# Second attention's way in: a projection in two parts, shared out over DVE, ACT and POOL

## The reference

```python
qkv = jnp.einsum('bsd,df->bsf', x, Wqkv) + bqkv          # 256 + 64 + 64 columns
q = qkv[..., :256].reshape(b, s, 32, 8)
k = qkv[..., 256:320].reshape(b, s, 8, 8)                # repeated 4 times
v = qkv[..., 320:].reshape(b, s, 8, 8)                   # repeated 4 times
attn = softmax(einsum('bqhd,bkhd->bhqk', q, k) / sqrt(8))
out = einsum('bhqk,bkhd->bqhd', attn, v).reshape(b, s, 256) @ Wo + bo
```

## Time and profile before

| | us |
|---|---|
| median of 3 runs (lowest, highest) | 669.72 (668.78, 669.96) |
| the profiled execution | 669.68 |
| its span, first to last instruction | 667.8 |
| TensorE, DVE, ACT, POOL busy | 617.4, 404.4, 325.1, 213.2 |
| mean granted TensorE clock | 0.986 of 2.4 GHz |
| maxima of the scores on DVE, L1744, 256 | 157.6 |
| exps on ACT, L1505, 256 | 138.0 |

### The profile page before, as it was taken

One profiled execution on the slowest core, in us unless ns is written; L12 is line 12 of the kernel. 1 busy time (PEld: TensorE's weight loads), 2 busy tenths in 40 slices (PEclk: granted clock), 3 DMA queues, 4 the chain that ended last, 5 costly groups with the idle time before them and its releaser, 6 DMA issues.

```text
span 667.8 us, 11795 instructions
## 1 busy us (share of the span) xinstructions
PE 617.4 (92%) x4298; PEld 408.0 (61%) x4298; DVE 404.4 (61%) x929; ACT 325.1 (49%) x645; POOL 213.2 (32%) x312
## 2 busy tenths in 40 slices
PE   3999999999999988799978999999999999989990
PEld 2887887887888785366665544444444445546660
DVE  4526705632760587533366999989998954743336
ACT  4523423433332224133215589898988875523322
POOL 5870561282073154513333031201010100331331
PEclk9999999999999999899989999999999999999996
DMA  6000200300199992222379994000000000031213
GB/s 220 33 1 33 96 1 20 107 1 1 38 283 299 78 314 77 78 58 81 105 237 346 303 180 3 1 1 2 2 1 2 1 2 1 9 104 55 81 56 126
DMA packets 69000, 57.40 MB, mean 86 GB/s; under 512 B 21520, under 2 KB 64400, under 8 KB 68944
## 3 DMA queue, kind: packets, MB, share of 16 engines
q1 hardware_dynamic: 66736, 50.60, 31.2%
q0 software_dynamic: 2208, 6.05, 2.5%
HBM read 30.78 MB, written 25.85 MB: 85 GB/s over the span
## 4 chain that ended last, share of the span: by engine, by line
PE 73%; DVE 16%; DMA 3%; ACT 3%; issue 2%; POOL 1%; SPq 1%; ACTq 0%; POOLq 0%; DVEq 0%
PE psum L303 9%; PE psum L305 8%; PE psum L304 8%; PE psum L1289 8%; PE psum L1634 8%; DVE mx L1744 7%; PE psum L1606 5%; PE psum L1318 5%; PE psum L1594 5%; PE psum L1619 3%; PE psum L1213 2%; DVE stat L666 2%; PE psum L1564 2%; PE psum L1282 2%; PE psum L1199 1%
## 5 line engine op out<-in xcount | busy, mean ns | idle before, releaser
L1744 DVE TENSOR_REDUCE mx<-psum 128x1 f32<-128x512 f32 x256 | 157.6, 681 | 17.6 <-PE psum L1606 17.5
L1505 ACT ACTIVATE pr<-psum 128x512 f32<-128x512 f32 x256 | 138.0, 598 | 27.9 <-PE psum L1619 26.1
L1634 PE MATMUL psum<-pr,vals 128*32 128x256 f32 x1024 | 77.6, 389 | 0.0
L1619 PE MATMUL psum<-qT,kT 32*128 32x512 f32 x256 | 76.6, 494 | 0.7 <-ACT pr L1505 0.7
L1606 PE MATMUL psum<-kT,qT 32*128 32x512 f32 x256 | 67.7, 488 | 1.7 <-ACT qT L1472 0.7
L1289 PE MATMUL psum<-w_gu,xgT 128*128 x120 | 56.4, 592 | 0.0
L624 POOL DMA_INDIRECT routed_y<-yr,xg x30 | 28.7, 958 | 86.1 <-DVE yr L876 85.5
L1606 PEld LDWEIGHTS psum<-kT,qT 32*128 32x128 f32 x256 | 26.3, 181 | 43.9 <-issue 21.4
L1546 POOL CAST mp<-mx 128x16 bf16<-128x16 f32 x16 | 3.1, 196 | 150.5 <-DVE mx L1744 150.5
L867 DVE SCALAR_TENSOR_TENSOR h<-psum,xg,sg 128x256 f32<-128x256 f32 x30 | 14.5, 484 | 49.8 <-ACT sg L1046 49.8
L1046 ACT ACTIVATE sg<-psum,xg 128x256 f32<-128x256 f32 x30 | 14.2, 474 | 60.4 <-PE psum L1289 60.4
(11 more groups left out here) (214 smaller groups left out, 1406.6 us busy)
## 6 DMA issues: line engine op xcount, KB each, us to landing
sorted_x<-zeros SPq DMA_DIRECT2D x2, 9088.0 KB, 39.2
w_gu<-in_L_ffn_gate_w SPq DMA_DIRECT2D x16, 256.0 KB, 6.2
w_gu<-in_L_ffn_up_w SPq DMA_DIRECT2D x16, 256.0 KB, 6.3
w_d<-in_L_ffn_down_w SPq DMA_DIRECT2D x16, 256.0 KB, 6.6
xg<-sorted_x SPq DMA_DIRECT2D x30, 129.0 KB, 2.2
wk_f<-in_L_attn_Wk SPq DMA_DIRECT2D x4, 512.0 KB, 5.2
wq_f<-in_L_attn_Wq SPq DMA_DIRECT2D x4, 512.0 KB, 6.0
wv_f<-in_L_attn_Wv SPq DMA_DIRECT2D x4, 512.0 KB, 3.7
```

The costliest lines, as they stand in the source:

```text
L1505: nc.scalar.activation(pr[d % 3][:, j], s2_bank(d, j), ACT.Exp, scale=SCALE).then_inc(exp_ready, 1)
L1619: mm(s2_bank(d, j), kT[n // GH][rows, kc * P:(kc + 1) * P], qT2[n % 2][rows, :], start=True, stop=True).then_inc(s2_made, 1)
L1634: last = mm(ps[AV_BANK][j * VW:(j + 1) * VW, cols], vals[:, n // NKV * TB + kc, n % NKV // GH * GH + j, :], pr[d % 3][:, j, cols], start=( ...
L1744: v.tensor_reduce(mx[n % 2][:, t, j:j + 1], s1_bank(c, j), AX.X, ALU.max, negate=True).then_inc(max_read, 1)
```

## The change

The projection of the first sequence's four tiles is split. project_first makes 128 columns: the keys (64) and the first eight heads' queries (64). DVE takes these with the bias (take_first), ACT makes their high parts, and DVE both low parts (first_low), the last two between the statistics of x; stats_x(1) moves behind the takes. project_rest makes the other 192 query columns and the 64 value columns, for tile 0 after the turn of q1, for tiles 1 to 3 in steps 0 to 2, in place of keep-warm matmuls. ACT copies them without the bias (take_rest); POOL adds the bias, makes high and low parts, and adds the values' bias as it copies them. In steps 3 to 6 ACT in place of DVE takes the second sequence's tiles (take), again without the bias, which POOL adds. complete(1) is split in three, in steps 3, 4 and 5. The second half's turned x goes through banks 6 and 7 in place of 4 and 6, and the turn in step 2 waits for its copies. Ahead of it all 25 keep-warm units become 18, a wait and 8. qkv and wqkv get 512 columns per tile, so that one access pattern reaches both parts of the first 128 columns; stack_hi and stack_lo get a range of heads.

```diff
+HALF = NQ * HD
+FH = 2 * GH
+FQ = FH * HD
...
-        TURN_X = ((4, 5, 6, 7), (0, 1, 0, 1), (0, 1, 4, 6), (0, 1, 0, 1))
+        TURN_X = ((4, 5, 6, 7), (0, 1, 0, 1), (0, 1, 6, 7), (0, 1, 0, 1))
...
                     else:
                         mark(ins)
-            def stats_x(half):
+            def stats_x(half, between=None):
                 for i in range(TB):
                     dve.wait_ge(dve_chain, sums_from[half] + i + 1)
                     tile_stats(x, half * TB + i)
+                    if between:
+                        between(i)
                 close_stats(0, half)
...
-            close_x(1, 1)
-            l1_y = dve_l1(dve, link, mark, settle, y_tiles, close_stats, sum_x)
+            sum_x(1, 1)
+            l1_y = dve_l1(dve, link, mark, settle, y_tiles, close_stats, sum_x, stats_x)
             stats_x(0)
             for t in range(TB, NT):
...
-            def complete(p):
-                for t in range(NT):
+            def complete(p, tiles=range(NT)):
...
             pe.wait_ge(y_ready, NT + 1)
-            keep_warm(25, 2)
+            keep_warm(18, 2)
+            pe.wait_ge(rstd_ready[1], 5)
+            keep_warm(8, 2)
             pe.wait_ge(var_ready[0], 10)
             keep_warm(5, 2)
...
+        REST_BANK = (3, 4, 3, 4)
...
+        def first_of(ap):
+            return ap.rearrange("p (a n) -> p a n", a=2)[:, :, 0:FQ]
...
-            def hi_parts(b, t):
-                act.wait_ge(qkv_ready, b * TB + t + 1)
-                stack_hi(nc.scalar, b, t, "k").then_inc(k_hi_made[b], 1)
-                stack_hi(nc.scalar, b, t, "q").then_inc(q_hi_made[b], 1)
+            def first_hi(t):
+                act.wait_ge(first_ready, t + 1)
+                stack_hi(nc.scalar, 0, t, "k").then_inc(k_hi_made[0], 1)
+                stack_hi(nc.scalar, 0, t, "q", (0, FH)).then_inc(q_hi_made[0], 1)
+            def take_rest(t):
+                act.wait_ge(rest_made, t + 1)
+                nc.scalar.activation(qkv[:, t, FQ:HALF], ps[REST_BANK[t]][:, 0:HALF - FQ], ACT.Copy)
+                nc.scalar.activation(qkv[:, t, KEND:QKV], ps[REST_BANK[t]][:, HALF - FQ:HALF], ACT.Copy).then_inc(qkv_ready, 1)
+            def take(t):
+                act.wait_ge(qkv_made, t + 1)
+                nc.scalar.activation(qkv[:, t, 0:QKV], ps[QKV_BANK[t]][:, 0:QKV], ACT.Copy).then_inc(qkv_ready, 1)
             act.wait_ge(l1_consts, L1_CONSTS)
             for t in range(TB):
-                hi_parts(0, t)
+                first_hi(t)
             for what in FIRST:
                 copy_turn(what)
+            take_rest(0)
             normalise(2, 1)
+            take_rest(1)
             for c in range(END):
                 d = c - LAG
+                if c == 1:
+                    take_rest(2)
                 if c == 2:
                     turn_copy(2, 2)
                     turn_copy(2, 3)
-                    complete(1)
+                if c == QKV_AT:
+                    take_rest(3)
+                if QKV_AT <= c < min(QKV_AT + TB, LAG):
+                    take(TB + c - QKV_AT)
+                    if c + 1 < QKV_AT + TB:
+                        complete(1, range(NT)[(c - QKV_AT) * NT // 3:(c + 1 - QKV_AT) * NT // 3])
                 n = (c - 12) // TB if c % TB == 0 and c >= 12 else -1
                 if 0 <= n < NG:
                     act.wait_ge(av_done, (n + 1) * TB)
...
                     if 0 <= d < STEPS:
                         act.wait_ge(s2_made, s2_no(d, j) + 1)
                         nc.scalar.activation(pr[d % 3][:, j], s2_bank(d, j), ACT.Exp, scale=SCALE).then_inc(exp_ready, 1)
+                if LAG <= c < QKV_AT + TB:
+                    take(TB + c - QKV_AT)
...
+            def add_bias(t, cols):
+                g.tensor_tensor(qkv[:, t, cols], qkv[:, t, cols], bqkv[:, cols], ALU.add).then_inc(biased, 1)
             for t in range(TB):
-                pool.wait_ge(q_hi_made[0], t + 1)
-                stack_lo(g, 0, t, "q").then_inc(q_stacked[0], 1)
+                pool.wait_ge(qkv_ready, t + 1)
+                add_bias(t, slice(FQ, HALF))
+                pool.wait_ge(biased, t + 1)
+                stack_hi(g, 0, t, "q", (FH, NQ)).then_inc(rest_hi, 1)
+                pool.wait_ge(rest_hi, t + 1)
+                stack_lo(g, 0, t, "q", (FH, NQ)).then_inc(q_stacked[0], 1)
             def values(b):
                 tiles = slice(b * TB, (b + 1) * TB)
-                g.tensor_copy(vals[:, tiles, :, 0:HD],
-                              qkv[:, tiles, KEND:QKV].rearrange("p t (g d) -> p t g d", d=HD)).then_inc(vals_ready, 1)
+                g.tensor_tensor(vals[:, tiles, :, 0:HD], qkv[:, tiles, KEND:QKV].rearrange("p t (g d) -> p t g d", d=HD),
+                                bqkv[:, KEND:QKV].rearrange("p (g d) -> p g d", d=HD).unsqueeze(1).to_broadcast([P, TB, NKV, HD]),
+                                ALU.add).then_inc(vals_ready, 1)
             values(0)
             def second_batch(t):
                 pool.wait_ge(qkv_ready, TB + t + 1)
+                add_bias(TB + t, slice(0, KEND))
+                pool.wait_ge(biased, TB + t + 1)
...
+            def columns(o, t, cols):
+                for c in range(KC):
+                    last = mm(o, xT[:, c, t * P:(t + 1) * P], cols(wqkv[:, c]), start=(c == 0), stop=(c == KC - 1))
+                return last
+            def project_first(t):
+                pe.wait_ge(xT_ready, 4 * 2 + t // 2 + 1)
+                columns(ps[QKV_BANK[t]][:, 0:2 * FQ], t,
+                        first_of).then_inc(qkv_made, 1)
+            def project_rest(t):
+                if t >= 2:
+                    pe.wait_ge(qkv_ready, t - 1)
+                columns(ps[REST_BANK[t]][:, 0:HALF - FQ], t, lambda w: w[:, FQ:HALF])
+                columns(ps[REST_BANK[t]][:, HALF - FQ:HALF], t, lambda w: w[:, KEND:QKV]).then_inc(rest_made, 1)
             def project_qkv(t):
                 pe.wait_ge(xT_ready, 4 * 2 + t // 2 + 1)
-                if t >= TB:
-                    pe.wait_ge(qkv_ready, t if t == NT - 1 else TB)
-                for c in range(KC):
-                    last = mm(ps[QKV_BANK[t]][:, 0:QKV], xT[:, c, t * P:(t + 1) * P], wqkv[:, c],
-                              start=(c == 0), stop=(c == KC - 1))
-                last.then_inc(qkv_made, 1)
+                pe.wait_ge(qkv_ready, t if t == NT - 1 else TB)
+                columns(ps[QKV_BANK[t]][:, 0:QKV], t, lambda w: w[:, 0:QKV]).then_inc(qkv_made, 1)
             def turn(what):
                 n = TURNS.index(what)
...
                     wait_bank(pe, what)
                 elif n >= 2:
                     wait_read(pe, TURNS[n - 1])
+                    pe.wait_ge(xT_ready, 4 * 2 + 4)
                 else:
-                    pe.wait_ge(qkv_ready, TB)
+                    pe.wait_ge(first_stacked, TB)
                 into = ps[bank_no(what)]
                 kind, i = what
                 b, u = divmod(i, 2 if kind == "k" else NKV)
...
                 elif kind == "k":
                     pe.wait_ge(k_stacked[b], TB)
                 else:
-                    pe.wait_ge(q_stacked[b], TB)
+                    if i * GH < FH:
+                        pe.wait_ge(first_stacked, TB)
+                    else:
+                        pe.wait_ge(q_stacked[b], TB)
                     if kind == "q2":
                         pe.wait_ge(max_ready, i + 1)
                 for t in range(TB):
...
             turn_x(2, range(2))
             for t in range(TB):
-                project_qkv(t)
-            pe.wait_ge(qkv_ready, TB)
-            keep_warm(3, 3)
+                project_first(t)
+            keep_warm(4, 3)
             turn(FIRST[0])
-            keep_warm(4, 3)
+            keep_warm(2, 3)
             turn(FIRST[1])
+            project_rest(0)
             for c in range(END):
                 d = c - LAG
                 if c == 2:
                     turn_x(2, range(2, 4))
                 if c < STEPS:
                     scores1(c, 0)
-                if c < QKV_AT:
-                    keep_warm(2, 3)
+                if c < 2:
+                    project_rest(c + 1)
                 if 0 <= d < STEPS:
                     scores2(d, 0)
                 if 0 <= d - 2 < STEPS and (d - 2) % TB:
...
                         if what[1] == NG - 1:
                             keep_warm(2, SPARE)
                         turn(what)
-                if c < QKV_AT:
-                    keep_warm(2, 3)
+                if c < 2:
+                    keep_warm(2, AV_BANK)
+                if c == 2:
+                    project_rest(3)
                 if 0 <= d < STEPS:
...
-            def take(t):
+            def take_first(t):
                 dve.wait_ge(qkv_made, t + 1)
-                v.tensor_tensor(qkv[:, t, :], ps[QKV_BANK[t]][:, 0:QKV], bqkv[:], ALU.add).then_inc(qkv_ready, 1)
-            def key_lo(t):
```

(45 more changed lines are left out.)

3 lines of the change are left out of this document (1 added, 2 removed).

## The result

| | before | changed |
|---|---|---|
| median of 20 runs each (lowest, highest), us | 674.02 (668.78, 677.6) | 676.41 (673.13, 680.23) |
| ratio, 95% interval | | 1.0057 (1.0038, 1.0075) |
| the profiled execution, us | 669.68 | 676.85 |
| its span, us | 667.8 | 675.1 |
| its mean granted clock | 0.986 | 0.970 |

The ratio is the one on record; the medians differ by 2.4 us and the means by 3.1 ± 1.3 us. Of all runs told of here one, the slowest of e3, lay over 1.5% above the fastest of its kernel, and is left out of e3's ratio and means.

A forecast was written before the change was run, and what follows sets the result against it. The stretch from the way in to the first loop steps was taken as serial, TensorE carrying 73% of the span. A 2.5 us lead, all but 0.1 lost to q2's late copy, gave 669.68 - 0.1, set at 669.5; range 668.3 to 671.1.

The forecast's parts named there:

- The base: Whole kernel: profiled execution 669.68 us and median 669.72 before the change, both given the same forecast, 669.5.
- The way in: First projections to first scores: smaller pieces bring first scores to 359.35 against 362.19, a lead of 2.85 us.
- rival 3: DVE's low parts at the way in cost 0.35 each, first_stacked at 358.5, total 671.0 us; chance 0.05.
- Steps 0 to 2: Loop start: steps 0 and 1 take 2.27 us each, with project_rest 1.0 and warmers 0.43; step 2 ends at 367.6.
- The stall on the copy: Step 5: ACT copies q2 only after take(6) and three tiles of x; scores2(0, 0) at 377.85, TensorE idle about 2 us.
- the lead: Time gained: 2.85 us at first scores, 2.5 at the end of project_qkv(6), 0.1 left at scores2(0, 0).
- What follows "is as before": After scores2(0, 0): exps, project_qkv(7) and maxima at the same distances as before, first weigh at 385.2.
- the gap on the way in: TensorE idle 1.6 us from 355.4, after four warmers and before turn k; full clock expected to hold.
- Rival 2: Clock falls after the 1.6 us idle at 355.4, losing 1.9 us in steps 0 and 1: 671.4 us; chance 0.09.
- two counter-examples: Against the clock falling: stretches busy 1.14 and 0.44 of 2.00 us, read as 1.56 idle, kept the full clock.
- DVE relieved of the takes: Steps 3 to 6: DVE loses four takes of 0.55 us; the time saved is idle, about 2 us before its 27th maximum.
- Rival 1: Step 5: q2's copy does not come behind project_qkv(6), so the 2.5 us lead is kept: 667.2 us; chance 0.08.

The follow-up runs named there:

- e3: Kernel before, with ACT in step 5 waiting for tile 6's projection and completing four tiles of x before copying q2: ratio 1.0084, mean +4.6 ± 1.7 us.
- e1: Changed kernel, but in step 5 ACT copies q2 before taking tile 6 and completing x: ratio 1.0011 to the kernel before.
- e2: Changed kernel with nine keep-warm units filling TensorE's idle time just ahead of scores2(0, 0): ratio 1.0015 to the kernel before, mean +1.6 ± 0.9 us.
- e5: e4 with DVE again taking the second sequence's tiles with the bias, POOL adding none to them: ratio 0.9986 to the kernel before.
- e4: e1 with x completed in steps 3 and 4, four tiles each: ratio 0.9981 to the kernel before, first weigh at 33.90 against 34.98 in e1.
- e6: e4 with weights ordered queries, values, keys, so a tile's rest is one block of 256 columns: ratio 0.9978 to the kernel before.

## Why the prediction was wrong, point by point

- **The base: the larger part of the miss.** The forecast was 669.5, the measured median 676.41, 6.9 us more. 4.3 of them are the kernel before itself, whose median went from 669.72 in three runs to 674.02 in twenty; I had taken three runs within 0.2% as its spread, and it spreads over 1.4%, by the clock. The other 2.6 are the change's: forecast 0.2 below the base's median, it came 2.4 above, and that by itself lies outside the range, 1.4 us to either side of the old base.
- **The way in: right.** First scores 9.29 after the normalisation, forecast 9.23; first_stacked, the price of the low parts (0.22, so rival 3 fell) and POOL's share came as priced: the last low part starts 354.80 and the turn follows at 355.08. That the sum fits to 0.06 is in part luck: first_stacked came 0.16 earlier than forecast, the two turns with their warmers took 1.54 for 1.35. The sixteen first pieces took 2.07 for 1.78, in DVE's cover. The row that decided this was the low part of 0.22 in the earlier trace rows. What the Trainium skill says in SBUF — State Buffer, "SBUF: two separate sides", of the shared port pair was not put to the test further: no POOL instruction ran beside these.
- **Steps 0 to 2: a term mis-sized.** project_rest was forecast at 1.0 us and the first took 1.04, but behind a pair of scores it takes 1.24, and four warmers there take 0.64 and not 0.43. The same 0.2 stands in the chain of waits of the kernel before, four warmers behind scores against eight behind a turn:

```profile
360.18 0.89 PE psum L1128 x8
...
362.69 0.64 PE psum L1128 x4
```

  By the eight, four are 0.44. I had taken that price for all and not looked at the row where they follow scores, 32 rows high. Two such returns from scores to full height in step 0, two in step 1 and one in step 2, with 0.04 on each rest, make 1.1 of the 1.25 us by which tile 6's projection was later than forecast.
- **The stall on the copy: right in mechanism and in length.** 1.92 us of idle, the queue behind it as told. With the term above the lead was not only spent but overdrawn: scores2(0, 0) 1.2 later than before, where 0.1 earlier was forecast. e1 adds that completing x would have held the first exp anyway, a second hold-up on the same instructions that the prediction did not see.
- **What follows "is as before": this step failed.** I had asked of the clock only at the gap on the way in (forecast 1.6 us, measured 1.22), where it held, and not at the stall that I had found myself. There a stretch with TensorE half busy was followed by 13.7 us at 1.2 GHz. Rival 2 had the cause, with 0.09, but at the wrong stretch, and priced it at 1.9 us, by one fall of 3.4 us; here it cost 4.7 to 5.0 in the profile. One of its two counter-examples was misread as well: 1.14 us busy of 2.00 leaves 0.86 idle, so that only the other was as empty as the gap. e3 (the stall alone, in the old kernel: 4.6 ± 1.7 us for 2.4 of delay) and e2 (the stall filled: 1.9 ± 1.4 us less with no instruction earlier) show from both sides that the stall costs more than its length. Of the changed kernel's 3 to 4 us, 1.2 are the delay of scores2(0, 0), and the rest, by that difference about 2 to 3, goes with the clock.
- **DVE relieved of the takes: right that it is idle.** e5 shows that undoing it costs nothing.
- Rival 1's kept lead needed what no edit of the diff had: the copy and x out of the way. e4 shows 1.2 us of it, e6 1.9.

## What to carry to other kernels

When a change puts a wait on TensorE, price what the clock does behind it, not the wait alone, and ask it of each stretch that the change empties, not of the first. Lay out what the in-order engine has ahead of the one copy that the next stage waits for; here three tiles of work that nobody was waiting for stood ahead of it. Price an instruction by a row in which it follows the same neighbour: here 0.2 us hung on what stood ahead. And compare kernels by many runs with the clock beside each: at equal clock two kernels may be alike and still differ in how often they have it.

## What the runs showed of the hardware

- The same program's time goes with the granted clock: 669.7 us at a mean of 0.986 and 675.8 at 0.973, in 127 runs of the kernel before. Which executions lose the clock, and where, varies; how often they do differs from kernel to kernel, as counted above.
- From the first exp to the 65th, 3.4 us at 1.2 GHz cost 1.5 to 1.8 us, 6.8 us cost 2.8 to 2.9 and 13.7 us cost 5.0.
- What stands behind scores (32 rows high) took longer than the same pieces behind matmuls of full height: 1.24 against 1.04 us for the eight pieces of a rest, 0.64 against 0.44 for four warmers, 0.59 against 0.44 for a turn of four, 1.49 against 1.36 for a tile of 384 columns (5.44/4 in the earlier trace rows). Why is not shown.
- Four pieces of 192 and four of 64 columns in float32 take 1.04 us, four of 256 0.86.
- ACT copies 192 and 64 columns from PSUM in 0.33 and 0.22 us. DVE low parts of 128x64 follow each other in 0.13 us when POOL is idle, against 0.35 beside POOL's own in the earlier trace rows.
